# Untiled in place of column-tiled products in the attention stage of a decoder layer

## The chip, the cores and the metric

The kernel runs on one core of a Trainium2 chip, as one launch. The metric is the device time of the execution in microseconds (us): the median of the runs shown. TensorE (PE in the profile; its weight loads are the row PEld) does all the matrix products. VectorE is DVE, ScalarE is ACT, GpSimd is POOL, SyncE is SP.

## The reference, cut to what matters

Tokens: 4 sequences of 512, width 512, in float32. Three sublayers, each on a layer-normed input and added to x:

```python
def _L0_attn_ref(...):          # the "mixer"
    xn = x * rsqrt(mean(x*x) + EPS) * w_norm
    proj = einsum('bld,td->blt', xn, W_in)         # z, xi, dt, B, C
    xi = silu(causal_conv4(xi)); dt = softplus(dt + dt_bias)
    h_t = exp(dt * A) * h_{t-1} + dt * mean_head(xi) * B ; y_t = sum(h_t * C)
    y = einsum('blh,ih->bli', y, W_h2i) * silu(z)
    return einsum('bli,di->bld', y, W_out) + residual

def _L0_xattn_ref(q, k, v):     # k = v = ctx; 32 query heads, 8 key heads, head width 16
    weights = softmax(einsum('bkgsd,bktd->bkgst', qh, kh) / 4)
    return einsum('bkgst,bktd->bkgsd', weights, vh)

def _L0_ffn_ref(...):           # shared expert, and 2 of 16 routed experts per token
    shared = silu(x @ shared_gate_w) * (x @ shared_up_w) @ shared_down_w
    routed = sum_e comb[:, e] * (silu(x @ g_e) * (x @ u_e)) @ down_e
    return shared + routed

x = x + _L0_attn_ref(_layernorm(x), ...)
x = x + _L0_xattn_ref(_layernorm(x), ctx, ctx)
x = x + _L0_ffn_ref(_layernorm(x), ...)
```

## The kernel before, in words

The program has two phases. `stream_phase` does the mixer, the attention and the shared expert of the first three sequences, and `experts_phase` (which the diff does not touch) does the shared expert of the last sequence and the routed experts.

`stream_phase` is an order written out by hand. It is cut into slots, from -92 to 263, and every engine goes through the same slots with its own queue; semaphores tie the queues together. Slot s from 0 to 255 is one step of the attention. There are 32 pairs of sequence and key head, of 8 slots each. In TensorE's queue a slot holds, in this order:

- `scores(s)` (L1167): two bf16 products of 512 moving columns into `ps_s`, 99 rows of contraction. It waits (L1173) until ScalarE has taken the exponential of the slot before out of the same `ps_s` (L892, `prob<-ps_s`).
- transposes of keys, queries and tokens, at fixed slots (L1034, L1041, L1074), and `outputs` (L1067).
- the first half of the mixer's work for this slot (`mixer_half`, L1155): one float32 product of 512 columns (`project`, L1112, or `project_out`, L1136), or one bf16 product (`heads_to_inner`, L1122), or nothing.
- `max_scores(s + 12)` (L1180): the same scores turned the other way, two bf16 products of 96 rows into `ps_m`. It waits (L1190) until VectorE has reduced the slot before out of `ps_m` (L683, `mx<-ps_m`).
- the second half of the mixer's work, and once for each sequence `head_means` (L1055).
- `front` (L1215), from slot 164 on: transposes, router products and the shared expert's products of one sequence.
- `transpose_max` (L1048) in one slot of eight, four products of 12 columns.
- in every odd slot `products` (L1197): the probabilities times the values, 16 float32 products of 128 moving columns.

The mixer's work runs 92 slots ahead: that of the first sequence lies before slot 0, that of the last ends at slot 163.

Some products fill only 32 columns of the stationary operand and are always laid into column tiles of the array with `tile_position=(0, 32 j)`: `products` (L1209), `head_means` (L1062), `project_steps` (L1107), the router's (L1234). Four of these, one in each column tile, are a quad below. The transposes of 128 columns (L1038, L1045, L1081, L1225) are never tiled.

All other products of the phase go through one helper, `product` (L1019). Before slot 0 it issues one untiled product (L1022 in the profile). From slot 0 on `tiled[0]` is true, and it issues four products of 32 stationary columns, one in each column tile (L1024). A float32 product stands in the trace as two passes, so a float32 call of `product` is 8 records when tiled and 2 when not, and a bf16 one is 4 or 1.

Of the kernel before, what the change touches and what calls it, by code (L numbers as in the profile page):

```python
# [15 lines left out]
P = 128  # L16
# [28 lines left out]
def stream_phase(nc, dram, x1, score, ident, identb, kept, out):  # L45
# [42 lines left out]
    with ExitStack() as ctx:  # L88
# [128 lines left out]
        def fronting(slot):  # L217

            at = slot - FRONT
            return [(a, at - WINDOW * a) for a in range(B - 1) if -6 <= at - WINDOW * a < WINDOW]  # L220
# [10 lines left out]
        def mixing(slot):  # L231

            return divmod(slot + LEAD, PERIOD)

        def batch_at(slot, at):

            b, off = divmod(slot - at, PERIOD)
            return b if off == 0 and 0 <= b < B else None
# [775 lines left out]
        @block.tensor  # L1014
        def _(pe):
            taken = []
            tiled = [False]

            def product(dst, stationary, moving, start, stop):  # L1019

                if not tiled[0]:
                    return nc.tensor.matmul(dst, stationary, moving, start=start, stop=stop)  # L1022
                for c in range(0, P, 32):
                    ins = nc.tensor.matmul(dst[c:c + 32, :], stationary[:, c:c + 32], moving, start=start, stop=stop,  # L1024
                                           tile_position=(0, c))
                return ins

            def claim(done, value):

# [4 lines left out]
            def transpose_keys(b):  # L1034
                pe.wait_ge(s_ctx, 16 * (b + 1))
                claim(s_prest, 5 * b + 1)
                for t in range(TB):
                    ins = nc.tensor.transpose(ps_t[:, t * P:(t + 1) * P], keys[:, t, :], ident[:, :])  # L1038
                ins.then_inc(s_ptr, 1)

            def transpose_queries(b, c):  # L1041
                pe.wait_ge(s_q, TB * (b + 1))
                claim(s_prest, 5 * b + c + 2)
                for t in range(TB):
                    ins = nc.tensor.transpose(ps_t[:, t * P:(t + 1) * P], q[:, t, c * P:(c + 1) * P], ident[:, :])  # L1045
                ins.then_inc(s_ptr, 1)
# [8 lines left out]
            def head_means(b):  # L1055
                pe.wait_ge(s_xs, KI * (b + 1))
                if b == 0:
                    pe.wait_ge(s_rest, 16 * 3)
                claim(s_gain, b + 1)
                for i in range(KI):  # L1060
                    for j in range(4):
                        ins = nc.tensor.matmul(ps_t[32 * j:32 * j + 32, 0:P], head_mean[:, i, :],  # L1062
                                               xz[:, i, j * P:(j + 1) * P], start=(i == 0), stop=(i == KI - 1),
                                               tile_position=(0, 32 * j))
                ins.then_inc(s_mean, 1)

            def outputs(b):  # L1067
                pe.wait_ge(s_hc, NS * (b + 1))
                claim(s_yrest, b + 1)
                for k in range(NS):  # L1070
                    ins = product(ps_t[:, :], state_sum[:, k, :], csb[:, k, :], start=(k == 0), stop=(k == NS - 1))
                ins.then_inc(s_y, 1)

            def transpose_tokens(b, j):  # L1074
                pe.wait_ge(s_ln, TB * b + j + 1)
                if b:
                    claim(s_xnT, TB * b + j + 1)
                turned = four[j] if b == 0 else ps_t[:, :]
                for k in range(KD):
                    rows = first_xn[j] if b == 0 else xt[:, j, :]  # L1080
                    ins = nc.tensor.transpose(turned[:, k * P:(k + 1) * P], rows[:, k * P:(k + 1) * P], ident[:, :])  # L1081
                ins.then_inc(s_tr, 1)
# [72 lines left out]
            def mixer_half(b, m, h):  # L1155
                at = 2 * m + h
                if at == 0:
                    project_steps(b)
                elif 4 <= at < 4 * GROUPS:
                    project(b, m // 2, at % 4)  # L1160
                elif H2I_AT <= at < H2I_AT + KI:
                    heads_to_inner(b, at - H2I_AT)
                elif OUT_AT <= at < OUT_AT + TB * KI:
                    j, i = divmod(at - OUT_AT, KI)
                    project_out(b, j, i)

            def scores(slot):  # L1167
                n, u = divmod(slot, UNITS)
                g, t = n % G, u // 2
                if u == 0:  # L1170
                    pe.wait_ge(s_mrow, 48 * (n + 1))
                if slot:
                    pe.wait_ge(s_exp, slot)  # L1173
                for i in range(2):
                    r = u % 2 * 2 + i
                    ins = product(ps_s[:, i, :], k_stack[:, g, t * P:(t + 1) * P], q_stack[:, g * R + r, :],
                                  start=True, stop=True)
                ins.then_inc(s_sc, 1)

            def max_scores(m):  # L1180
                n, u = divmod(m, UNITS)
                b, g = divmod(n, G)
                if u == 0 and g % 2 == 0:
                    pe.wait_ge(s_qst[g // 2], 96 * (b + 1))
                if u == 0 and g % 4 == 0:
                    pe.wait_ge(s_kst[g // 4], 96 * (b + 1))
                if m == 0:
                    pe.wait_ge(s_ones, 1)
                if m:
                    pe.wait_ge(s_max, m)  # L1190
                for i in range(2):
                    r, t = u // 2, 2 * (u % 2) + i
                    ins = product(ps_m[:, i, :], q_stack[0:KQ, g * R + r, t * P:(t + 1) * P], k_stack[0:KQ, g, :],
                                  start=True, stop=True)
                ins.then_inc(s_mm, 1)

            def products(p):  # L1197
                n, t = divmod(p, TB)
                g = n % G
                pe.wait_ge(s_exp, 2 * p + 2)  # L1200
                if t == 0:
                    if n:
                        pe.wait_ge(s_otc, n)
                    pe.wait_ge(s_val, n + 1)
                for r in range(R):
                    weights = prob[:, (2 * p + r // 2) % PROB, r % 2, :].rearrange("p (t a i) -> p a t i", a=4, i=VW)
                    for a in range(4):
                        out_rows = ps_o[a * VW:(a + 1) * VW, r * P:(r + 1) * P]
                        ins = nc.tensor.matmul(out_rows.rearrange("p (t i) -> p t i", i=VW), values[:, t, g, :],  # L1209
                                               weights[:, a, :, :], start=(t == 0 and r == 0),  # L1210
                                               stop=(t == TB - 1 and r == R - 1),
                                               tile_position=(0, a * VW))
                ins.then_inc(s_pv, 1)
# [61 lines left out]
            for slot in span:  # L1275
                b, m = mixing(slot)
                n, u = divmod(slot, UNITS)
                tiled[0] = slot >= 0
                if 0 <= slot < SLOTS:
                    scores(slot)  # L1280
                if (a := batch_at(slot, K_AT)) is not None:
                    transpose_keys(a)
                for c in range(4):
                    if (a := batch_at(slot, C_AT[c])) is not None:
                        transpose_queries(a, c)
                if b < B and m == Y_AT[b]:
                    outputs(b)
                if b + 1 < B and m in TURN_AT:
                    transpose_tokens(b + 1, TURN_AT.index(m))
                if b < B:  # L1290
                    mixer_half(b, m, 0)
                if 0 <= slot + AHEAD < SLOTS:
                    max_scores(slot + AHEAD)
                if b < B:
                    mixer_half(b, m, 1)
                if b < B and m == 30:
                    head_means(b)
                if slot == SLOTS:
                    products(SLOTS // 2 - 1)
                for a, r in fronting(slot):  # L1300
                    front(a, r)
                if u == 5 and 0 <= n + 1 < N:
                    transpose_max(n + 1)
                if 3 <= slot < SLOTS and slot % 2 == 1:
                    products((slot - 3) // 2)
# [703 lines left out]
```

## Time and profile before

| | |
|---|---|
| median of 3 runs | 1221.38 us (1219.46 to 1221.67) |
| profiled execution, its own time | 1216.94 us |
| its span, first to last instruction | 1215.1 us |
| granted TensorE clock, mean | 0.999 |
| TensorE busy | 1168.5 us (96%), 13185 matmul records |
| VectorE busy | 691.5 us (57%) |
| ScalarE busy | 475.3 us (39%) |
| GpSimd busy | 386.6 us (32%) |

The busy time of an engine is the time in which at least one of its instructions is under way. Matmuls overlap each other, so a busy TensorE can still have short waits in it. Times in the rows are us from the start of the span; "mean ns" is the mean duration of one instruction.

### The profile page before, as it was taken

How to read it: one execution, taken by the hardware profiler on the slowest of the kernel's cores; microseconds unless marked ns; L12 is line 12 of the kernel's file. 1: busy time of each engine (PE TensorE's matmuls, PEld its weight loads, DVE VectorE, ACT ScalarE, POOL GpSimd, SP SyncE). 2: the span in 40 equal slices, each digit the busy share in tenths (PEclk: the TensorE clock that was granted, in tenths of full speed). 3: DMA queues.
4: the chain of work that ended last, by engine and by line, in shares of the span. 5: the costliest groups of instructions: out<-in, count | busy, mean ns of one | idle time of the engine just before them, and what ended most of it. 6: DMA issues, size and time to landing. Idle time of an engine off the chain costs nothing. (4 is left out here: it accounts for less than half of the span.)

```text
span 1215.1 us, 31305 instructions
## 1 busy us (share of the span) xinstructions
PE 1168.5 (96%) x13185; PEld 581.4 (48%) x13186; DVE 691.5 (57%) x1150; ACT 475.3 (39%) x669; POOL 386.6 (32%) x502
## 2 busy tenths in 40 slices
PE   6999999999999999999999999999999999999997
PEld 3444434444545544545645554444444444444443
DVE  3833595756787665668675777877657222222221
ACT  3320324533555453545453455555632222222222
POOL 5212311221321330231122121110102576777775
PEclk9999999999999999999999999999999999999999
DMA  8321874104384201364500245200135676678640
GB/s 205 103 80 32 190 161 120 29 15 120 69 162 85 72 25 28 84 118 105 112 20 16 68 105 93 83 3 3 72 114 166 171 188 138 142 225 233 182 83 2
DMA packets 119603, 122.24 MB, mean 101 GB/s; under 512 B 25472, under 2 KB 84992, under 8 KB 119344
## 3 DMA queue, kind: packets, MB, share of 16 engines
q1 hardware_dynamic: 101744, 98.59, 31.6%
q0 software_dynamic: 17008, 21.16, 9.0%
q8 instruction: 99, 1.62, 0.6%
q10 hardware_dynamic: 720, 0.61, 0.2%
q14 instruction: 32, 0.26, 0.1%
HBM read 94.63 MB, written 40.77 MB: 111 GB/s over the span
## 5 line engine op out<-in xcount | busy, mean ns | idle before, releaser
L683 DVE TENSOR_REDUCE mx<-ps_m 128x2 f32<-128x1024 f32 x256 | 313.0, 1223 | 193.6 <-PE ps_m L1024 189.3
L892 ACT ACTIVATE prob<-ps_s 128x1024 f32<-128x1024 f32 x256 | 262.0, 1023 | 322.7 <-PE ps_s L1024 321.7
L1024 PE MATMUL acc<-xnT,wring 128*32 128x512 f32 x1888 | 249.0, 592 | 0.6 <-DVE first_z L619 0.6
L1869 PE MATMUL ps_gu<-ring,xgT 128*128 x376 | 176.7, 593 | 1.0 <-DVE xgT L1573 1.0
L1508 POOL DMA_INDIRECT out<-y,dest x92 | 143.7, 1562 | 77.5 <-ACT y L1734 60.4
L1024 PE MATMUL ps_s<-q_stack,k_stack 99*32 99x512 bf16 x2048 | 161.7, 380 | 4.4 <-ACT prob L892 3.8
L1024 PE MATMUL ps_m<-k_stack,q_stack 96*32 96x512 bf16 x1952 | 153.2, 380 | 9.8 <-DVE mx L683 8.2
L1573 DVE COPY xgT<-ps_x 128x512 f32<-128x512 f32 x47 | 32.5, 692 | 202.1 <-PE ps_x L1839 202.1
L1209 PE MATMUL ps_o<-prob,values 128*32 128x128 f32 x4096 | 138.4, 273 | 0.0
L1209 PEld LDWEIGHTS ps_o<-prob,values 128*32 128x32 f32 x4096 | 116.3, 110 | 44.7 <-issue 39.2
L1024 PEld LDWEIGHTS ps_m<-k_stack,q_stack 96*32 96x32 bf16 x1952 | 55.6, 96 | 127.3 <-issue 72.8
L1869 PEld LDWEIGHTS ps_gu<-ring,xgT 128*128 128x128 f32 x376 | 67.7, 190 | 68.2 <-issue 68.1
L1024 PEld LDWEIGHTS ps_s<-q_stack,k_stack 99*32 99x32 bf16 x2048 | 58.9, 96 | 77.6 <-issue 41.5
L1885 PE MATMUL acc<-ring,hT 128*128 x188 | 88.6, 593 | 0.9 <-ACT hT L1725 0.9
L1022 PE MATMUL acc<-xnT,wring 128*128 128x512 f32 x184 | 84.5, 597 | 2.1 <-DVE xz L601 2.0
L1024 PEld LDWEIGHTS acc<-xnT,wring 128*32 128x32 f32 x1888 | 65.8, 109 | 43.1 <-issue 6.1
L1024 PE MATMUL acc<-wring,xz 128*32 128x512 f32 x576 | 76.5, 593 | 0.0
L429 POOL TENSOR_SCALAR mneg<-mx 128x16 f32<-128x16 f32 x32 | 10.1, 317 | 195.7 <-DVE mx L683 195.7
L1734 ACT ACTIVATE y<-acc,share 128x512 f32<-128x512 f32 x47 | 32.3, 687 | 83.3 <-PE acc L1885 83.3
L601 DVE SCALAR_TENSOR_TENSOR xz<-acc,convw,xz 128x511 f32<-128x511 f32 (+2 forms) x84 | 62.7, 746 | 2.9 <-ACT xz L973 0.9
L1497 POOL DMA_INDIRECT xg<-xn_rows,token x47 | 48.5, 1031 | 27.9 <-DVE token L1651 13.9
L415 POOL COPY values<-keys 128x64 f32<-128x64 f32 x32 | 9.2, 299 | 142.2 <-PE ps_o L1209 142.2
(282 smaller groups left out, 1201.6 us busy)
## 6 DMA issues: line engine op xcount, KB each, us to landing
ring<-in_w_experts SPq DMA_DIRECT2D x96, 256.0 KB, 4.7
wring<-in_w_in SPq DMA_DIRECT2D x80, 256.0 KB, 4.2
q_stack<-part_rows SPq DMA_DIRECT2D x96, 128.0 KB, 4.6
wring<-in_w_out SPq DMA_DIRECT2D x32, 256.0 KB, 2.9
part_rows<-part SPq DMA_DIRECT2D x20, 384.0 KB, 3.8
out<-x SPq DMA_DIRECT2D x4, 1024.0 KB, 4.8
xt<-in_x SPq DMA_DIRECT2D x14, 256.0 KB, 4.6
k_stack<-part_rows SPq DMA_DIRECT2D x48, 64.0 KB, 3.0
```

Source lines behind the costliest of these rows:

```text
L601: ins = nc.vector.scalar_tensor_tensor(out=xz[:, i, tap:], in0=bank(b, 5 + i)[:, :SEQ - tap], scalar=convw[:, i, 3 - tap:4 - tap], in1=xz[ ...
L683: nc.vector.tensor_reduce(mx[:, n % G, 2 * u:2 * u + 2], ps_m[:, :, :], AX.X, ALU.max).then_inc(s_max, 1)
L892: nc.scalar.activation(prob[:, slot % PROB, :, :], ps_s[:, :, :], ACT.Exp, scale=SCALE).then_inc(s_exp, 1)
L1022: return nc.tensor.matmul(dst, stationary, moving, start=start, stop=stop)
L1024: ins = nc.tensor.matmul(dst[c:c + 32, :], stationary[:, c:c + 32], moving, start=start, stop=stop, tile_position=(0, c))
L1209: ins = nc.tensor.matmul(out_rows.rearrange("p (t i) -> p t i", i=VW), values[:, t, g, :], weights[:, a, :, :], start=(t == 0 and r == 0), ...
L1497: pool.indirect_dma_start(out=xg[:, n % XG, :], out_offset=None, in_=xn_rows[:, :], in_offset=bass.IndirectOffsetOnAxis(ap=token[:, n:n + ...
L1508: pool.indirect_dma_start(out=out[:, :], out_offset=bass.IndirectOffsetOnAxis(ap=dest[:, k, n:n + 1], axis=0), in_=y[:, n % YB, :], in_off ...
L1573: nc.vector.tensor_copy(xgT[:, p, :], ps_x[p][:, :]).then_inc(s["txc"], 1)
L1734: nc.scalar.activation(y[:, n % YB, :], ps_y[p][:, :], ACT.Copy, scale=share[:, n:n + 1]).then_inc(s["yc"], 1)
L1869: ins = nc.tensor.matmul(ps_gu[p][:, :], xgT[:, p, k * P:(k + 1) * P], weights(own)[:, k * 2 * F:(k + 1) * 2 * F], start=(k == 0), stop=(k ...
L1885: ins = nc.tensor.matmul(ps_y[p][:, :], hT[:, p, k * P:(k + 1) * P], weights(own)[:, WUP + k * D:WUP + (k + 1) * D], start=(k == 0), stop= ...
```

## The change

The helper loses its tiled form. From slot 0 on the products of `scores`, `max_scores`, `outputs`, `project`, `heads_to_inner`, `project_out` and the shared expert in `front` are issued as one product over all 128 stationary columns, as they already are before slot 0. The products that name a `tile_position` themselves (L1062, L1107, L1209, L1234) and `transpose_max` stay as they are. Order, waits, buffers and transfers stay as they are.

```diff
         def _(pe):
             taken = []
-            tiled = [False]
 
             def product(dst, stationary, moving, start, stop):
 
-                if not tiled[0]:
-                    return nc.tensor.matmul(dst, stationary, moving, start=start, stop=stop)
-                for c in range(0, P, 32):
-                    ins = nc.tensor.matmul(dst[c:c + 32, :], stationary[:, c:c + 32], moving, start=start, stop=stop,
-                                           tile_position=(0, c))
-                return ins
+                return nc.tensor.matmul(dst, stationary, moving, start=start, stop=stop)
...
             for slot in span:
                 b, m = mixing(slot)
                 n, u = divmod(slot, UNITS)
-                tiled[0] = slot >= 0
                 if 0 <= slot < SLOTS:
                     scores(slot)
```

## Rows read from the trace of the kernel before

**Rows 1.** The page: the span in 40 slices, TensorE and its clock.

```profile
PE   6999999999999999999999999999999999999997
...
PEclk9999999999999999999999999999999999999999
```

**Rows 2.** Busy time of each engine from slot 0 to the last probabilities-times-values product.

```profile
183.70:893.00 709.30, 691.66 (x11608) 356.46 (x11611) 493.18 (x669) 349.06 (x422) 141.05 (x288) 1.00 0.29 69
```

**Rows 3.** That stretch: the helper's line alone, and groups of matmuls with their counts.

```profile
183.70:893.00 709.30, 570.04 (x6892) 1.00 0.29 69
...
L1024 PE MATMUL ps_s<-q_stack,k_stack 99*32 99x512 bf16 x2048 | 161.7, 380 | 4.4 <-ACT prob L892 3.8
L1024 PE MATMUL ps_m<-k_stack,q_stack 96*32 96x512 bf16 x1952 | 153.2, 380 | 9.8 <-DVE mx L683 8.2
L1209 PE MATMUL ps_o<-prob,values 128*32 128x128 f32 x4096 | 138.4, 273 | 0.0
```

**Rows 4.** The chain of waits over that stretch: total us, times, longest.

```profile
PEld ps_m L1024 <- DVE mx L683: 48.1, 93, 1.5
...
PEld ps_s L1024 <- ACT prob L892: 35.0, 54, 1.2
```

**Rows 5.** Timeline of TensorE in a tiled stretch: start, us, instructions.

```profile
399.26 0.64 PE L1024 MATMUL ps_s<-q_stack,k_stack 99*32 99x512 bf16 x8
399.69 1.06 PE L1024 MATMUL acc<-xnT,wring 128*32 128x512 f32 x8
400.55 0.64 PE L1024 MATMUL ps_m<-k_stack,q_stack 96*32 96x512 bf16 x8
```

**Rows 6.** Timeline of TensorE in an untiled stretch, before slot 0.

```profile
163.96 0.60 PE L1022 MATMUL ps_m<-k_stack,q_stack 96*128 96x512 bf16 x2
164.41 1.88 PE L1022 MATMUL acc<-xnT,wring 128*128 128x512 f32 x4
```

**Rows 7.** Timeline: 16 quads (head_means, first sequence) between untiled products.

```profile
65.06 1.45 PE L1022 MATMUL ps_s<-xnT,wring 128*128 128x512 f32 x3
66.44 1.95 PE L1062 MATMUL ps_t<-xz,head_mean 128*32 128x128 f32 x64
68.32 1.13 PE L1022 MATMUL ps_s<-xnT,wring 128*128 128x512 f32 x2
```

**Rows 8.** Timeline: the same 16 quads (second sequence) between tiled products.

```profile
192.80 1.93 PE L1062 MATMUL ps_t<-xz,head_mean 128*32 128x128 f32 x64
194.54 0.61 PE L1024 MATMUL ps_s<-q_stack,k_stack 99*32 99x512 bf16 x8
```

**Rows 9.** Timeline: an untiled block (token transposes) between tiled products.

```profile
251.97 0.68 PE L1024 MATMUL ps_s<-q_stack,k_stack 99*32 99x512 bf16 x8
252.58 0.66 PE L1081 MATMUL ps_t<-ident,xt 128*128 128x128 f32 x4
253.17 1.06 PE L1024 MATMUL acc<-wring,xz 128*32 128x512 f32 x8
```

**Rows 10.** Timeline of all engines, slot 200: in brackets, idle before and releaser.

```profile
772.32 0.61 PE L1024 MATMUL ps_m<-k_stack,q_stack 96*32 96x512 bf16 x8 [0.40 <-DVE mx L683]
...
773.39 1.22 DVE L683 TENSOR_REDUCE mx<-ps_m 128x2 f32<-128x1024 f32 x1
```

**Rows 11.** Timeline: the first (slot 12) and the last (slot 238) of the 28 even slots with a wait.

```profile
224.11 0.64 PE L1024 MATMUL ps_s<-q_stack,k_stack 99*32 99x512 bf16 x8
224.64 1.07 PE L1024 MATMUL acc<-xnT,wring 128*32 128x512 f32 x8
...
853.65 0.68 PE L1024 MATMUL ps_s<-q_stack,k_stack 99*32 99x512 bf16 x8
854.51 0.61 PE L1024 MATMUL ps_m<-k_stack,q_stack 96*32 96x512 bf16 x8 [0.18 <-DVE mx L683]
```

**Rows 12.** Groups of untiled weight loads: line, shape, count, busy us, mean ns.

```profile
L1022 PEld LDWEIGHTS ps_s<-xnT,wring 128*128 128x128 f32 x80 | 15.1, 190 | 18.9 <-issue 18.9
...
L1022 PEld LDWEIGHTS ps_m<-k_stack,q_stack 96*128 96x128 bf16 x24 | 1.9, 97 | 8.4 <-DVE mx L683 7.0 <-issue 0.9
```

## The prediction

> **What bounds the kernel now.** I read the page first. TensorE is at 9 tenths or more in 38 of the 40 slices, and its clock is at the full level, 2.4 GHz, in all of them [rows 1]; the change does not lower the load, so I leave the clock out. Then I cut out the stretch that the change touches, slot 0 to the last `products`. Its 709.3 us hold 691.7 us of TensorE, 493 of VectorE and 349 of ScalarE [rows 2]. So TensorE sets the pace here, and what its queue gains or loses is passed on, except where it waits.
>
> How much does it wait? A busy share can't say, because matmuls overlap, so I add up what the array needs, from starts in the timeline. Two tiled bf16 products start 0.43 us before the next work (399.26 to 399.69), so one costs 0.216; a tiled float32 product of two passes costs 0.43 a pass (399.69 to 400.55 is two passes, 0.86) [rows 5]. One quad of 128 columns (four records, one pass) costs 0.109: 64 records, 16 quads, take 192.80 to 194.54, 1.74 us [rows 8]. In the stretch the helper's line has 6892 records; 2048 and 1952 of them are `scores` and `max_scores`, and 96 are the 24 bf16 calls of `heads_to_inner`; that leaves 2796 in float32, 699 quads at 0.43, 301 us. The bf16 ones are 1024 quads at 0.216, 222 us. `products` is 4096 records, 1024 quads at 0.109, 112 us [rows 2, 3]. That leaves 620 of the 11608 records: 88 quads and 144 transposes at 0.109, 25 us, and 124 small ones of `transpose_max`, at most 0.055 each where they follow one another, 7. The joins of the transposes, priced below, are 10. That is 677 us of 709: TensorE waits for about 32 us in small pieces. The chain of waits names them: weight loads of `ps_m` behind VectorE's reduction (93 times) and of `ps_s` behind ScalarE's exponential (54 times) [rows 4].
>
> **The product itself: no gain, no loss.** Four tiles run side by side: tiled pair 0.43 us [rows 5]; untiled pair, just after a wait, 163.96 to 164.41, 0.45 [rows 6]. A float32 pass is 0.43 in both (untiled: four passes last 1.88, that is 3 x 0.43 and the 0.59 of the last) [rows 5, 6]. A weight load of 128 columns takes 97 ns in bf16 and 190 in float32 [rows 12], less than the 216 and 430 under which it is hidden in the stream. If the true difference were 2 ns a quad in either direction, 1723 quads would make it 3.5 us; I take 0 and keep 3 for the range.
>
> Against that stands a rule. The Trainium skill, TensorE: Matmul & The Clock Gate, section Measured speedup vs the span model, counts about 4 ns for each further tile of a set, 12 a quad; as an estimate, 1723 quads would give back 21 us, where the rows say 0. Rows 5 start the work behind a full stream of quads on time, so I follow them and keep the rule's case as a rival.
>
> **What the change adds: joins between tiled and untiled work.** `products` stays tiled, everything around it becomes untiled. The trace has this join before slot 0, and its twin without a join afterwards. `head_means` of the first sequence stands between untiled products: the last of three passes from 65.06 starts at 65.92 and gives way at 66.35, but the quads start at 66.44, 0.09 late. The 16 quads then take 66.44 to 68.32, 1.88 us, where the same work between tiled neighbours takes 1.74: 0.14 more. The two passes behind last 1.13, where 0.43 + 0.59 = 1.02 is due: 0.11 more [rows 7, 8]. So a tiled block in untiled surroundings costs 0.34 us with float32 behind it. Behind `products` comes `scores`, bf16. No row shows that join. Its weight load is 97 ns against 190 for float32, and the untiled pair that starts behind a wait, its load not hidden either, loses 0.01 to 0.02 [rows 6, 12]. So I take 0.01 for the last term, 0.24 us a block; the upper bound is 0.34, the lower 0.23.
>
> Blocks, counted in the order of the program: `products` 128 times (the last two touch, so 127 blocks, `transpose_max` inside 31 of them), `head_means` 3, `project_steps` 2, router 3, one of these touching another: 134. 134 x 0.24 = 32.2 us. Five have float32 behind them (+0.5), and the 31 with `transpose_max` cost a little less, because the other tiles begin `products` meanwhile (-1): 31.7.
>
> **What it takes away.** Today every untiled transpose block from slot 0 on sits between tiled products. At 251.97 two bf16 products start, due to give way at 252.40; the transposes start at 252.58, 0.18 late, of which 0.08 is a tile that already ran late (0.68 for the group against 0.60 untiled) and is not the join's. They need 4 x 0.109, to 253.02, and the next starts at 253.17, 0.15 late, and loses 0.02 more as its load is exposed [rows 6, 9]. So 0.27 a block, by 38 blocks: 10.3 us. Gross: 31.7 - 10.3 = +21.4 us.
>
> The Trainium skill, TensorEngine Tiling (Array Packing), section Tiling Modes (Key Properties), says that changing the mode drains TensorE and changing only the tile does not. The trace agrees in kind: late at each change, on time between quads [rows 5, 7]. Taken literally, the next work would start when the last matmul ends, 0.16 late (0.59 less 0.43) and not 0.09: by some 190 more changes, +13 us on the sum. The 0.09 is measured, so the sum keeps it.
>
> **What the waits take back.** The two joins of a block lie between the `max_scores` of an odd slot and that of the next even slot. Where the latter waits today for VectorE's reduction of the former, which is set off ahead of the joins, the delay fits into the wait. Rows 10 show one: `ps_m` at 772.32 waited 0.40 us of an idle TensorE. I went through all 126 even slots for the excess between the start of `scores`, plus what stands behind it, and that of `max_scores`: 28 have more than 0.05 us, from slot 12 (224.11 + 0.43 = 224.54, but the next starts at 224.64) to slot 238 (853.65 + 0.43 = 854.08, but 854.51) [rows 11]. Capped at 0.24 each they hold 4.7 us: 1.4 up to slot 140, 3.3 from slot 164 on. The others have none, mostly because a float32 filler stands there.
>
> In odd slots the wait is mostly the loop itself (0.6 us of products, 1.22 of reduction, then the next), which moves along with TensorE; a late start hides nothing. But part of it is VectorE's backlog: the reduction started at 773.39, though its input was complete at 772.93 (772.32 + 0.61) [rows 10]. A later TensorE finds a shorter backlog. From slot 164 on about 10 such waits beyond the loop give up to 0.24 each, 1.9 us. Before 164 the waits are fewer and longer (up to 1.5 us by the row on `mx` [rows 4]; five or six a sequence, at the hand-over between sequences and around `heads_to_inner`); they are chains through ScalarE and VectorE that began one or two blocks earlier. I give them 0.24 each for about four of them, three sequences: 3. Ends: 0 and 6.
>
> Against it, six of the 38 removed blocks are `front`'s transposes in an even slot, followed by an odd slot's wait: what they give back only lengthens that wait, 6 x 0.27 = 1.6.
>
> Sum: 21.4 - 4.7 - 1.9 - 3 + 1.6 = **+13.4 us**. Nothing else moves: order, transfers, GpSimd and SyncE keep their work and are released a little later by TensorE; `experts_phase` starts later by the same amount.
>
> The profiled execution took 1216.94 us, 1.84 outside its span of 1215.1, so for a like run the sum gives 1230.3. The median of the runs is 4.4 higher, 1221.38: the forecast is 1234.8 us. Of a change of up to 0.2%, 2.4 us, this kernel's measurement can't tell it from none.
>
> **The rivals.**
> *The full bill* (chance 0.15): the waits in odd slots and the long ones are all loop and move along, so that nearly all of the gross stays: +19 to +25, say 1243. For it: 98 of the 126 even slots have no wait.
> *A dearer join into bf16* (0.04): it costs what the float32 one does, 127 x 0.10 = 12.7 more, 1247.
> *The waits take nearly all* (0.14, 0.03 of it within 0.2%): the 32 us of waits exceed the gross bill. If they take twice what I grant them, 4.7 + 1.9 + 3 = 9.6 more, +4 is left: 1225. For it: 147 waits of a weight load on the two engines [rows 4]. Against it: 98 even slots without one.
> *Faster* (0.04): the tiled products pay for their staggered tiles. A tiled pair lasts 0.64 us, at times 0.68, the untiled 0.60 [rows 5, 6, 9]. If each of 512 bf16 pairs paid 0.06, the change would save 31 us: 1221.4 - 31 + 21 = 1212. It decides from 0.042 a pair on. Against it: the work behind a tiled pair starts after 0.43 us, whatever the pair's length [rows 5].
>
> **How the numbers follow.** The forecast, +7 to +19, has 0.63 (1228 to 1240); with the full bill 0.15, the dear join 0.04, the absorbed 0.14, faster 0.04. Range: +5.6 to +22.6, 1227 to 1244, which leaves out the far parts of the rivals. Slower by over 0.2%: 0.93; within: 0.03; faster: 0.04.
>
> **What would show it.** In the new profile `ps_o` (L1209) stands between untiled products; each block starts 0.09 late and its successor `ps_s` starts some 0.14 late, and the 8 quads of `products` take 1.01 us from their start to the next in place of 0.87. In 304 to 425 us two slots lengthen by nearly 0.24, and slots 164 to 240 by less. The helper's 6892 records become 1723. The prediction is wrong if `ps_s` behind `ps_o` shows another delay, or if waits on `mx` and `prob` shrink by much more than 10 us.

## The result, and the profile after

The changed kernel takes 1235.33 us (median of 4 runs, 1234.09 to 1237.09); the kernel before took 1221.0 in the same comparison. The ratio is 1.012, with a 95% interval of 1.0103 to 1.0138: slower, by 12.6 to 16.8 us. The forecast was 1234.8.

| | before | after |
|---|---|---|
| profiled execution, its own time, us | 1216.94 | 1237.09 |
| its span, us | 1215.1 | 1235.3 |
| TensorE busy, us, and matmul records | 1168.5, 13185 | 1189.4, 7982 |
| VectorE busy, us | 691.5 | 692.2 |

The two profiled executions lie 20.2 us apart, more than the medians. 3.5 us of that comes before slot 0, where the kernels are the same: the first `scores` starts at 183.8 before and at 187.3 after, and one cause, a slower clock, is shown in the last section. From there to slot 255 the changed kernel is 16.5 us longer, and it ends about as late as it was at slot 255 (20.2 us against 20.0). I read the stretch from slot 0 to slot 255, since it is the same instructions of the other engines in both.

Busy time by stretch of the changed kernel, from the start of slot 0 to that of 160 and from there to that of 255 (engines in the order PE, PEld, DVE, ACT, POOL, then clock, DMA share, GB/s):

```profile
187.30:696.90 509.60, 500.24 (x4170) 246.06 (x4175) 336.79 (x419) 232.44 (x288) 106.37 (x201) 1.00 0.31 69
696.90:908.90 212.00, 204.66 (x2198) 98.45 (x2195) 155.81 (x250) 115.49 (x133) 34.86 (x87) 1.00 0.25 60
```

The same slots in the kernel before:

```profile
183.80:679.80 496.00, 486.62 (x7876) 253.03 (x7879) 336.00 (x418) 232.32 (x288) 106.12 (x201) 1.00 0.32 72
679.80:888.90 209.10, 200.84 (x3653) 100.85 (x3648) 155.81 (x250) 115.70 (x133) 34.93 (x87) 1.00 0.25 62
```

The other engines do the same work. The first 160 slots are 13.6 us longer (0.085 a slot), the last 95 only 2.9 (0.031 a slot), though `products` stands in every odd slot of both. Slot by slot, measured from one start of `scores` to the next, of the 79 odd slots from 3 to 159, 67 grew by 0.22 to 0.27 us, 11 of the others hold a transpose block that lost its joins, and one (157) grew by 0.18.

What a product costs has not moved. Timeline of TensorE in the changed kernel, slots 64 and 65:

```profile
392.67 0.60 PE L1020 MATMUL ps_m<-k_stack,q_stack 96*128 96x512 bf16 x2
393.10 1.02 PE L1020 MATMUL acc<-xnT,wring 128*128 128x512 f32 x2
393.96 0.59 PE L1020 MATMUL ps_s<-q_stack,k_stack 99*128 99x512 bf16 x2
394.40 1.02 PE L1020 MATMUL acc<-xnT,wring 128*128 128x512 f32 x2
395.26 0.59 PE L1020 MATMUL ps_m<-k_stack,q_stack 96*128 96x512 bf16 x2
```

and the same work, tiled, in the kernel before:

```profile
384.08 0.68 PE L1024 MATMUL ps_m<-k_stack,q_stack 96*32 96x512 bf16 x8
384.51 1.10 PE L1024 MATMUL acc<-xnT,wring 128*32 128x512 f32 x8
385.37 0.68 PE L1024 MATMUL ps_s<-q_stack,k_stack 99*32 99x512 bf16 x8
385.81 1.10 PE L1024 MATMUL acc<-xnT,wring 128*32 128x512 f32 x8
386.67 0.68 PE L1024 MATMUL ps_m<-k_stack,q_stack 96*32 96x512 bf16 x8
```

From one `ps_m` to the next but one: 392.67 to 395.26 untiled, 384.08 to 386.67 tiled, 2.59 us both. A group lasts 0.08 us less untiled (0.60 against 0.68), and nothing starts earlier for it.

What is new stands around `products`. The changed kernel, one block without and one with `transpose_max`:

```profile
403.97 1.02 PE L1020 MATMUL acc<-xnT,wring 128*128 128x512 f32 x2
404.92 1.08 PE L1203 MATMUL ps_o<-prob,values 128*32 128x128 f32 x32
405.93 0.61 PE L1020 MATMUL ps_s<-q_stack,k_stack 99*128 99x512 bf16 x2
406.37 1.02 PE L1020 MATMUL acc<-xnT,wring 128*128 128x512 f32 x2
...
410.26 1.02 PE L1020 MATMUL acc<-xnT,wring 128*128 128x512 f32 x2
411.21 0.33 PE L1046 MATMUL ps_t<-identb,mpart 128*12 128x128 bf16 x3
411.33 0.31 PE L1203 MATMUL ps_o<-prob,values 128*32 128x128 f32 x3
411.38 0.22 PE L1046 MATMUL ps_t<-identb,mpart 128*12 128x128 bf16 x1
411.43 1.04 PE L1203 MATMUL ps_o<-prob,values 128*32 128x128 f32 x29
412.40 0.60 PE L1020 MATMUL ps_s<-q_stack,k_stack 99*128 99x512 bf16 x2
```

Two float32 passes from 403.97 are due to give way at 404.83; `ps_o` starts at 404.92, 0.09 late. Its 8 quads are due to give way after 0.87; `ps_s` starts after 1.01, 0.14 late. The pair of `scores` then takes 0.44 in place of 0.43. That is the 0.24 us of rows 7 and 8, with the small last term that no row of before showed. The same two paths from `acc` to `ps_s` in the kernel before, first without `transpose_max` and then with it (lines between left out):

```profile
387.10 1.10 PE L1024 MATMUL acc<-xnT,wring 128*32 128x512 f32 x8
...
388.83 0.68 PE L1024 MATMUL ps_s<-q_stack,k_stack 99*32 99x512 bf16 x8
...
427.24 1.04 PE L1024 MATMUL acc<-xnT,wring 128*32 128x512 f32 x8
...
429.12 0.68 PE L1024 MATMUL ps_s<-q_stack,k_stack 99*32 99x512 bf16 x8
```

Without: 1.96 us now, 1.73 before. With: 2.14 now, 1.88 before. `transpose_max` adds 0.18 now and added 0.15. (A reason that would fit is that its one busy tile ran on behind the others, since the group after it lasts 0.68; no run tests it.) With the 0.01 behind the join such a block costs 0.27 to 0.28, not a little less than 0.24.

The other kind of block has lost its joins. Transposes in the changed kernel, and in the kernel before:

```profile
733.57 0.59 PE L1020 MATMUL ps_s<-q_stack,k_stack 99*128 99x512 bf16 x2
734.00 0.60 PE L1039 MATMUL ps_t<-ident,xz 128*128 128x128 f32 x4
734.44 0.60 PE L1020 MATMUL ps_m<-k_stack,q_stack 96*128 96x512 bf16 x2
```

```profile
716.27 0.61 PE L1024 MATMUL ps_s<-q_stack,k_stack 99*32 99x512 bf16 x8
716.82 0.66 PE L1045 MATMUL ps_t<-ident,xz 128*128 128x128 f32 x4
717.41 0.62 PE L1024 MATMUL ps_m<-k_stack,q_stack 96*32 96x512 bf16 x8
```

From `ps_s` to `ps_m` it is 0.87 us now and was 1.14: 0.27 less. Where the tiled group ahead of the transposes lasted 0.68 and not 0.62, it is more. The block of rows 9 in the changed kernel:

```profile
257.66 0.61 PE L1020 MATMUL ps_s<-q_stack,k_stack 99*128 99x512 bf16 x2
258.10 0.60 PE L1075 MATMUL ps_t<-ident,xt 128*128 128x128 f32 x4
258.54 1.02 PE L1020 MATMUL acc<-wring,xz 128*128 128x512 f32 x2
```

It takes 0.88 from `ps_s` to `acc`, and took 1.20: 0.32 less. Ten of the 19 blocks ahead of slot 160 are of this kind.

### The profile page after: what moved, and what is told of

It reads as the page before. It is cut to its first block and busy times, and to the rows that moved or that the text cites. A ratio compares the mean times of both kernels' runs of the same rounds, so it can differ in the third digit from the quotient of the medians.

```text
span 1235.3 us, 20906 instructions
## 1 busy us (share of the span) xinstructions
PE 1189.4 (96%) x7982; PEld 574.5 (47%) x7990; DVE 692.2 (56%) x1150; ACT 475.1 (38%) x669; POOL 387.8 (31%) x502
## 5 line engine op out<-in xcount | busy, mean ns | idle before, releaser
L683 DVE TENSOR_REDUCE mx<-ps_m 128x2 f32<-128x1024 f32 x256 | 313.1, 1223 | 207.1 <-PE ps_m L1020 204.4
L1020 PE MATMUL acc<-xnT,wring 128*128 128x512 f32 x656 | 326.8, 596 | 2.8 <-DVE xz L601 2.0
L1020 PE MATMUL ps_m<-k_stack,q_stack 96*128 96x512 bf16 x512 | 153.0, 380 | 8.5 <-DVE mx L683 7.2
L1020 PEld LDWEIGHTS acc<-xnT,wring 128*128 128x128 f32 x656 | 123.1, 191 | 79.8 <-issue 37.1
L1020 PE MATMUL ps_s<-q_stack,k_stack 99*128 99x512 bf16 x512 | 153.9, 382 | 5.4 <-ACT prob L892 5.3
L1203 PEld LDWEIGHTS ps_o<-prob,values 128*32 128x32 f32 x4096 | 106.0, 109 | 61.6 <-issue 48.8
L1020 PEld LDWEIGHTS ps_m<-k_stack,q_stack 96*128 96x128 bf16 x512 | 45.1, 97 | 132.5 <-issue 69.0
L1020 PE MATMUL acc<-wring,xz 128*128 128x512 f32 x168 | 84.6, 592 | 0.0
L1020 PEld LDWEIGHTS ps_s<-q_stack,k_stack 99*128 99x128 bf16 x512 | 35.2, 97 | 101.6 <-issue 65.5
L419 POOL CAST part<-rest 128x512 bf16<-128x512 f32 x20 | 13.4, 670 | 125.3 <-DVE rest L676 125.3
```

Of the source, the lines that this page charges most:

```text
L683: nc.vector.tensor_reduce(mx[:, n % G, 2 * u:2 * u + 2], ps_m[:, :, :], AX.X, ALU.max).then_inc(s_max, 1)
```

## The experiments

Eight kernels. The edits are to the first kernel or to the changed one; medians stand beside that of the first kernel on the same chip. The changed kernel itself was run beside the first one only for the result above, so a distance between its median and one of these is only good to some 1.6 us, by which the first kernel's median moved from one sample to another; the traces are closer.

**Fewer blocks, the same products** (`e1_batch_untiled`, `e2_batch_tiled`). Both kernels with this edit, and at slot 256 the last two calls together:

```diff
-                if 3 <= slot < SLOTS and slot % 2 == 1:
+                if 5 <= slot < SLOTS and slot % 4 == 1:
+                    products((slot - 3) // 2 - 1)
                     products((slot - 3) // 2)
```

The changed kernel with it:

> The changed kernel, but the probabilities-times-values products are issued two calls at a time, in every fourth slot, so that the blocks between untiled products are halved (some 70 in place of 134); instructions and waits are the same. Theory of the joins (0.24 us a block): about 15 us less joins than in the changed kernel, and 5 us (3 to 8) slower than the tiled kernel with the same pairing. Rival, that the untiled product itself is dearer: as far above its tiled twin as the changed kernel is above the first one, 14 us. The pairing itself may cost some 12 us in both, because three light slots in a row wait for VectorE.

The first kernel with it:

> The first kernel (tiled products) with the same pairing of the probabilities-times-values products. No join is added or removed. Both theories: slower than the first kernel by what the pairing costs, 5 to 15 us, nearly all of it behind slot 164. It is the twin against which the untiled one with pairing is read.

Measured: 1248.67 us untiled (ratio to the first kernel 1.0242, 1.0221 to 1.0263) and 1244.17 tiled (1.0193, 1.0163 to 1.0222), the first kernel 1219.64. With the blocks halved, untiled is 4.5 us above tiled, where the changed kernel is 14.3 above the first one in its own comparison (15.7 above this sample of it): as the joins say, and not as a dearer product would have it. Untiled, then tiled, in two stretches each:

```profile
186.10:695.50 509.40, 493.03 (x4138) 249.07 (x4143) 335.80 (x417) 232.30 (x288) 104.38 (x201) 1.00 0.31 69
695.50:918.90 223.40, 204.91 (x2226) 101.74 (x2224) 158.01 (x251) 115.45 (x133) 34.79 (x87) 1.00 0.24 57
```

```profile
185.40:690.30 504.90, 489.35 (x7845) 243.00 (x7848) 336.90 (x417) 232.33 (x288) 104.93 (x201) 1.00 0.31 71
690.30:914.20 223.90, 207.36 (x3677) 103.58 (x3670) 158.09 (x251) 115.71 (x133) 34.88 (x87) 0.98 0.23 58
```

Up to slot 160 the difference is 4.5 us (509.4 against 504.9), at full clock in both. Behind it the untiled one is 0.5 shorter, but there TensorE's clock was at half in the tiled run for 6.8 us:

```profile
703.70:710.50 6.80, 6.49 (x79) 3.91 (x81) 5.32 (x13) 2.68 (x4) 2.64 (x4) 0.50 0.11 45
```

It covers slots 164 and 165, and these two alone are 2.3 us shorter in the untiled kernel; the other slots behind 160 are 1.9 us longer. At a like clock the traces thus lie some 6.4 us apart, still within the 3 to 8 of the joins and far from 14. All four tiled runs had a lower mean clock (0.992 to 0.995) than three of the four untiled ones (0.998), so the 4.5 between the medians is rather too small. The pairing itself costs 24.5 us in the tiled kernel, more than the 5 to 15 expected: 14.8 of it behind slot 160 (223.9 against 209.1, some 2 of it the clock), and 8.9 ahead of it. I had left the second out.

**Half of the slots** (`e3_untiled_from_128`): the first kernel with

```diff
-                tiled[0] = slot >= 0
+                tiled[0] = 0 <= slot < 128
```

> Products tiled in slots 0 to 127 as before, untiled from slot 128 on. Theory that joins are paid where TensorE has no wait and absorbed where it waits for VectorE: +6.4 us over the first kernel (this half's part of the difference between the two traces), less than half of the whole, although it holds half of the joins. Rival, that the bill goes by the number of products or joins alone: +8.

Measured: 1225.36 us, 5.7 above the first kernel's 1219.64 (ratio 1.005, 1.0033 to 1.0068). In the trace the slots from 128 to 255 take 313.7 us:

```profile
581.80:895.50 313.70, 304.71 (x3041) 147.43 (x3039) 217.35 (x321) 158.67 (x185) 55.84 (x125) 1.00 0.22 54
```

against 307.4 in the first kernel (581.5 to 888.9): +6.3. The half with the waits of slots 164 to 240 pays less than its half of 16.5. The medians alone can't tell 6.4 from 8; the trace can. The 6.4 had been read from the trace of the changed kernel, so this run shows that the bill comes back in the same slots, whatever form the slots before them have.

**More joins, fewer untiled products** (`e4_max_tiled`): in the changed kernel

```diff
+                    tiled[0] = slot >= 0
                     max_scores(slot + AHEAD)
+                    tiled[0] = False
```

> The changed kernel with the max_scores products tiled again (0 to 243), all others untiled. Fewer untiled products, but some 440 more joins of each kind's pair: 716 changes of mode in place of 278. Theory of the joins: 68 us more than the changed kernel before waits absorb some, 60 to 85 us above the first kernel. Rival, that the untiled products themselves cost the time: faster than the changed kernel, since 488 of them are tiled again.

Measured: 1289.08 us, 69.4 above the first kernel and 53.8 above the changed one (ratio 1.0569, 1.0542 to 1.0595). Timeline around a tiled `ps_m`:

```profile
421.77 1.02 PE L1022 MATMUL acc<-xnT,wring 128*128 128x512 f32 x2
422.73 0.62 PE L1024 MATMUL ps_m<-k_stack,q_stack 96*32 96x512 bf16 x8
423.27 1.12 PE L1022 MATMUL acc<-xnT,wring 128*128 128x512 f32 x2
```

It starts 0.96 us after the float32 product, not 0.86, and the next one 0.54 later, not 0.43. The traces count 438 more changes of mode than the changed kernel, so one costs 0.12 us on average, where 68 us would be 0.155; the distance to the changed kernel is 43.1 us up to slot 160 and 10.7 behind it, where more is lost in waits. That a tiled product makes the kernel dearer here, as an untiled one did among tiled ones, leaves only the change of mode.

**Move the join in front of float32** (`e5_scores_tiled`): in the changed kernel

```diff
+                    tiled[0] = slot >= 4 and slot % 2 == 0
                     scores(slot)
+                    tiled[0] = False
```

> The changed kernel, with scores tiled again in even slots alone, right behind the tiled probabilities-times-values products. The number of joins stays (272 changes of mode, 278 in the changed kernel), but the change back to untiled now mostly falls in front of a float32 product, whose exposed weight load costs 0.10 us, and not a bf16 one (0.01). Theory of the joins with that term: 3 to 7 us slower than the changed kernel. Rival, that a join costs the same whatever follows: no difference. Rival, that the untiled product is dearer: faster than the changed kernel.

Measured: 1240.2 us (ratio to the first kernel 1.017, 1.0153 to 1.0187; first kernel 1219.86), 4.9 above the changed kernel's 1235.33 (6.0, if each is taken from the first kernel of its own comparison), with six changes of mode fewer. The row that makes the difference:

```profile
412.90 0.68 PE L1024 MATMUL ps_s<-q_stack,k_stack 99*32 99x512 bf16 x8
413.51 1.13 PE L1022 MATMUL acc<-xnT,wring 128*128 128x512 f32 x2
414.47 0.60 PE L1022 MATMUL ps_m<-k_stack,q_stack 96*128 96x512 bf16 x2
```

The two passes behind the join last 1.13 and give way after 0.96, not 0.86. What follows the change of mode sets its price, and the exposed part of its weight load accounts for it. The stretches bear it out: up to slot 160 this kernel takes 514.5 us, 4.9 more than the changed one; behind it, where the mixer's float32 products no longer stand behind `scores`, it takes 211.7 against 212.0.

**Take the cover away** (`e6_half_maxima_tiled`, `e7_half_maxima_untiled`): in both kernels

```diff
-                nc.vector.tensor_reduce(mx[...], ps_m[:, :, :], AX.X, ALU.max)
+                nc.vector.tensor_reduce(mx[...], ps_m[:, :, 0:SEQ // 2], AX.X, ALU.max)
```

> The first kernel (tiled), but VectorE takes the maxima over half of the keys only, so that its reduction is shorter and TensorE waits less for it (this leaves out half of the maximum; the softmax is shifted by another constant). Both theories: 8 to 20 us faster than the first kernel. It is the twin for the next run.

> The changed kernel with the maxima over half of the keys. Theory that the joins' bill is 23 us and VectorE's waits hide 6 of it: with these waits mostly gone, the distance to the tiled twin grows to 20 us (18 to 23), from 16.5 in the two traces. Rival, that the joins cost only 16 us and nothing is hidden: the distance stays at 14 to 17.

Measured: 1196.41 us tiled (ratio 0.9809, 0.9793 to 0.9826) and 1218.19 untiled (0.9986, 0.9975 to 0.9997), the first kernel 1219.86. The tiled one gained 23.4 us, more than the 8 to 20 expected. The reduction fell from 1223 ns to 689, and the waits of the weight loads of `ps_m` for it from 48.1 us to 6.4 (tiled, 12 waits left) and from 47.4 to 5.3 (untiled, 8 left):

```profile
L683 DVE TENSOR_REDUCE mx<-ps_m 128x2 f32<-128x512 f32 x256 | 176.5, 689 | 286.9 <-PE ps_m L1024 281.8 <-PE ps_m L1022 3.2 <-DVE gains L721 0.4
```

Tiled, then untiled, the same slots as above:

```profile
180.30:671.40 491.10, 485.55 (x7879) 264.80 (x7882) 252.31 (x419) 232.03 (x288) 105.42 (x201) 1.00 0.32 73
671.40:866.40 195.00, 192.16 (x3650) 104.23 (x3639) 112.57 (x249) 115.47 (x133) 34.96 (x87) 1.00 0.27 67
```

```profile
180.20:685.40 505.20, 498.96 (x4169) 246.44 (x4173) 252.60 (x419) 232.00 (x288) 104.41 (x201) 1.00 0.30 70
685.40:887.00 201.60, 198.38 (x2197) 101.59 (x2193) 112.75 (x249) 114.67 (x133) 34.80 (x87) 1.00 0.25 64
```

The distance is now 14.1 us up to slot 160 (it was 13.6) and 6.6 behind it (it was 2.9): 20.7 in all, 21.8 between the medians. So the same joins cost 4.2 us more once VectorE no longer holds TensorE up. The rival without absorption, 14 to 17, is out. Slot by slot it is direct: 15 even slots from 164 to 238 were 0.19 to 0.37 us shorter in the changed kernel than in the first; between the two kernels with the short reduction, 13 of them differ by 0.01 or less and two (214, 238) by 0.08. Nearly all of the 4.2 comes from behind slot 160 (3.7), so VectorE's reduction hid joins there and hardly ahead of it.

**Merge blocks** (`e8_merged_blocks`): the first kernel with

```diff
-                tiled[0] = slot >= 0
+                tiled[0] = slot >= 0 and slot not in (165, 167, 203, 205, 241, 243)
```

> The first kernel (tiled), but scores and max_scores of six slots (165, 167, 203, 205, 241, 243) are untiled. These slots lie between two untiled transposes with no tiled-only product between them, so that two untiled blocks become one: 6 blocks fewer, where the changed kernel adds 96. Theory of the joins: up to 6 x 0.27 = 1.6 us faster than the first kernel from slot 0 to slot 255 of the trace, some of it lost in the waits of odd slots, so 0.3 to 1.6 us; the median moves by less than can be told. Rival, that an untiled product is dearer by itself: a little slower.

Measured: 1219.0 us against 1219.38 (ratio 1.0004, 0.9993 to 1.0015): no difference. In the trace the stretch from slot 0 to slot 255 is 704.3 us, where it was 705.1, 0.8 less, inside the 0.3 to 1.6 of the joins. Slots 0 to 156, the same code in both, differ by less than 0.01 us each, and the 0.8 lies in slots 164 and 165 (0.15 together), 203, 205, 241 and 243 (0.16 each):

```profile
185.60:889.90 704.30, 686.40 (x11444) 354.54 (x11443) 491.76 (x667) 348.19 (x421) 141.29 (x288) 1.00 0.30 69
```

So these 24 untiled products in the tiled kernel cost nothing where they made no new join, and the blocks that they merged gave time back. It is worth too little to be measured as time of the whole. The one edit here that beats both kernels is the maximum over half the keys; for softmax it is only a shift, but it no longer bounds the exponent, so it is a means of this study and not a proposal.

## Why the prediction was right, and where its terms were off

**The bound.** TensorE set the pace up to slot 160, as read. Behind it VectorE's reduction held it in part, which the pair with the shorter reduction confirms. One sign that I had named says less than I thought: the waits on `mx` and `prob` hardly changed in the view of rows 4 (47.4 us in 116 waits and 35.5 in 57, where it was 48.1 in 93 and 35.0 in 54). That view counts idle time of the weight-load queue and not of the array; its 83 us are not the 32 us of waits that I had added up, and it can't show what the waits took back.

**The product itself, 0.** Confirmed: 2.59 us for the same work in both forms. The rival that the staggered tiles cost time (0.04) fell. The Trainium skill, TensorE: Matmul & The Clock Gate, section Measured speedup vs the span model, has some 4 ns for each further tile; in a full stream no trace here shows it: the same work takes 2.59 us in either form, where by that figure its 8 quads would differ by 0.10, as an estimate.

**The joins added, 31.7 us from 134 blocks at 0.24.** The price for a plain block came out at 0.24, and its pieces (0.09, 0.14, 0.01) too; taking the bf16 successor by the untiled pair behind a wait was right, and the dearer join into bf16 (0.04) fell. The mis-sized piece is `transpose_max`: I took 1 us off for 31 blocks, and each was 0.04 dearer than the plain one. The 0.5 us for five blocks with float32 behind them was misread: in the trace bf16 work stands behind them (`ps_s` behind `head_means`, `ps_m` behind `project_steps`), and their slots grew by 0.20 to 0.28 us. The trace has 135 blocks, none of them touching another, 134 of them before slot 255. In place of 31.7: 103 x 0.24 + 31 x 0.28 = 33.4.

**The joins removed, 10.3 us.** I had set 0.08 us of rows 9 aside as a tile's that ran late anyway, and priced a block at 0.27. That holds for a block behind a group of 0.62; in the ten behind a late tile, that of rows 9 among them, 0.32 came back, most of the 0.08 with it. With the 0.01 of exposed load before the next work, 28 x 0.28 and 10 x 0.34 (the slots show 0.34) give 11.2. Gross +22.2, forecast 21.4.

**What the waits take back, net 8.0 us.** The measured figure is a remainder, the bill by the prices above less what the trace grew: 22.2 - 16.5 = 5.7. From slot 160 on the trace has 50 tiled blocks, 11 of them with `transpose_max`, and 19 transpose blocks fewer with joins: 39 x 0.24 + 11 x 0.28 - 19 x 0.28 = 7.1 us, and the stretch grew by 2.9; 4.2 were hidden, where I had 3.3 + 1.9 - 1.6 = 3.6. With the short reduction 6.6 of the 7.1 are paid, so VectorE's reduction is shown as what hid them. Ahead of slot 160 I had 1.4 for even slots and 3 for long waits, 4.4 in all; 22.2 - 7.1 - 13.6 = 1.5 were hidden, 0.6 of it in the even slots 12, 14, 76, 78, 140 and 142. This is the term that failed by most: the long waits around the hand-over gave back at most 0.9 of the 3, and moved along with TensorE for the rest. Their length was no evidence of slack. A reason that fits is that what they wait for is itself set off by TensorE one slot earlier; I read that from the order of the queues, and no run isolates it. The short reduction changed little here (14.1 us paid, 13.6 before), so what holds back the 1.0 that is still missing stays open.

So the +13.4 of the forecast stands against 16.5 in the stretch of the two traces: 0.8 short in the gross and 2.3 too much for the waits. Of the medians, 1235.33 against 1221.0 makes 14.3; against the later and larger samples of the first kernel (1219.4 to 1219.9) it is 15.5 to 16. That the forecast 1234.8 is within 0.6 us of the measured time is partly luck: the sum was 2 to 3 us short, and the first median, 1221.38, was some 1.5 to 2 us high.

**The full bill** (0.15) and **the waits take nearly all** (0.14) bracket it: 5.7 of 22.2 us were taken. **The dearer join into bf16** would have shown as 0.34 us a block and did not.

## What to carry to other kernels

On an engine that is busy all the time, count the changes between tiled and untiled matmuls, not the tiles: here each cost about 0.1 us with what its first weight load exposed on top, and the products cost the same in either form. If one kind of work must be tiled and comes often, tile everything around it; a form is cheap or dear by its neighbours. Price a join twice, once with the waits behind it and once without, since a faster reduction uncovered 4 us of joins here.

## What the runs showed of the hardware that was not expected

The granted clock fell to half, from 2.4 to 1.2 GHz, for some 3 us in the profiled run of the changed kernel, well ahead of the change:

```profile
96.10:98.90 2.80, 2.48 (x8) 0.99 (x6) 1.63 (x3) 1.15 (x3) 1.74 (x3) 0.50 0.00 0
```

Just before, TensorE had short single products with idle time between them:

```profile
94.06 0.39 PE L1020 MATMUL ps_s<-y_parts,wh2i 128*128 128x512 bf16 x1 [1.41 <-DVE xz L619]
...
95.84 0.61 PE L1020 MATMUL acc<-y_parts,wh2i 128*128 128x512 bf16 x1 [0.31 <-DVE xz L624]
96.24 1.06 PE L1032 MATMUL ps_t<-ident,keys 128*128 128x128 f32 x4
```

The kernel before has the same products with about the same gaps, at a clock of 1.00 throughout. The transposes took 0.85 us from their start to the next, at full clock 0.44. The slower clock is a small part of the 3.5 us by which the changed kernel's profiled run was late at slot 0; the rest came before, with the first loads, and is chance as far as the traces tell. In the tiled kernel with pairing the clock fell to half in this place too, for 6.8 us, and once more at 703.7 (its row stands with that experiment), behind a `ps_m` that had waited 1.23 us for VectorE.
